# Moving casts from VectorE to ScalarE and GpSimd ahead of the attention units, and the order of a few small steps in a fused attention and expert kernel

## The reference

```python
x = x + xattn(layernorm(x), ctx)      # x: 4 x 1024 x 256, ctx: 4 x 64 x 192, 16 heads of 16
#   q = xn @ Wq + bq;  k = ctx @ Wk + bk;  v = ctx @ Wv + bv
#   softmax(clip(q k^T * scale, -1e4, 1e4)) @ v @ Wo + bo
#   (all probabilities become 1/64 if any of them is NaN)
x = x + ffn(layernorm(x))             # shared SwiGLU plus 8 experts of hidden size 512, top 2
```

## Time and profile before

| | |
|---|---|
| median of 3 runs | 696.8 us (696.21 to 697.24) |
| the profiled execution | 694.34 us, its span 692.6 us |
| PE busy | 606.9 us (88%) |
| DVE busy | 422.7 us (61%) |
| ACT busy | 344.7 us (50%) |
| POOL busy | 393.1 us (57%) |
| granted PE clock, mean | 0.926 |

### The profile page before, as it was taken

How to read it: one execution, slowest core, us unless ns; L and a number is a source line. 1 busy time by engine, 2 the same in 40 slices (tenths; PEclk the granted TensorE clock), 3 DMA queues, 4 the chain that set the end, 5 groups by cost and what they waited for, 6 DMA issues and landing times.

```text
span 692.6 us, 15435 instructions
## 1 busy us (share of the span) xinstructions
PE 606.9 (88%) x5212; PEld 413.3 (60%) x5212; DVE 422.7 (61%) x920; ACT 344.7 (50%) x567; POOL 393.1 (57%) x330
## 2 busy tenths in 40 slices
PE   3597688999987896998898999999999999999990
PEld 1243234565554563554665678778788878787870
DVE  5999974987785652889945444454444454444440
ACT  3986376786768762565145334243333333333330
POOL 6598588887662112432126544656666667656643
PEclk9999855997759998999999999999999999999996
DMA  8443302152118899595219764566575667665633
GB/s 266 88 77 76 130 1 33 32 139 44 35 25 191 160 185 292 145 175 146 69 54 175 122 91 73 101 98 105 90 115 86 100 97 103 100 100 86 101 41 37
DMA packets 121102, 72.44 MB, mean 105 GB/s; under 512 B 91779, under 2 KB 114246, under 8 KB 121030
## 3 DMA queue, kind: packets, MB, share of 16 engines
q1 hardware_dynamic: 101974, 44.01, 29.4%
q0 software_dynamic: 19056, 27.43, 24.8%
HBM read 29.47 MB, written 22.15 MB: 75 GB/s over the span
## 4 chain that ended last, share of the span: by engine, by line
PE 58%; DVE 16%; DMA 8%; SPq 6%; ACT 5%; issue 4%; POOL 2%; POOLq 0%; DVEq 0%; ACTq 0%
PE bank L1517 56%; SPq L547 4%; DVE bank L1116 3%; DMA out<-w_stage,map_i 3%; DVE arena L1063 2%; DMA arena<-arena 2%; DMA qx<-qx 2%; PE bank L1876 1%; ACT arena L809 1%; DVE arena L1180 1%; DVE hidden L1411 1%; DVE bank L1417 1%; POOL out L739 1%; DMA qx<-arena 1%; POOL arena L636 1%
## 5 line engine op out<-in xcount | busy, mean ns | idle before, releaser
L1517 PE MATMUL bank<-arena 128*128 128x34 f16 (+6 forms) x1282 | 139.7, 253 | 23.7 <-DVE bank L1116 7.9
L1517 PE MATMUL bank<-qx,arena 128*128 128x256 f16 (+1 forms) x1584 | 157.9, 290 | 2.8 <-ACT hidden L869 1.2
L739 POOL DMA_INDIRECT out<-w_stage,map_i x71 | 113.8, 1602 | 72.3 <-DMA out<-w_stage,map_i 37.1
L1517 PEld LDWEIGHTS bank<-qx,arena 128*128 (+1 forms) x1584 | 126.7, 102 | 24.4 <-issue 8.9
L1517 PEld LDWEIGHTS bank<-arena 128*128 128x128 f16 (+2 forms) x1282 | 77.5, 107 | 74.7 <-issue 41.3
L726 POOL DMA_INDIRECT qx<-rows_d,map_i x71 | 73.3, 1033 | 78.1 <-DVE lane_w L1478 35.7
L1486 DVE TENSOR_TENSOR hidden<-bank,hidden 128x512 f32<-128x512 f32 x71 | 49.1, 692 | 108.0 <-ACT hidden L995 108.0
L1517 PE MATMUL bank<-arena,w_stage 128*128 x852 | 104.7, 273 | 1.7 <-ACT w_stage L1001 1.2
L995 ACT ACTIVATE hidden<-bank 128x512 f32<-128x512 f32 x71 | 42.4, 597 | 126.9 <-PE bank L1517 126.9
L1517 PE MATMUL bank<-qx,w_sh 128*128 128x512 f16 x384 | 91.1, 384 | 9.8 <-DVE hidden L1411 7.5
L1517 PEld LDWEIGHTS bank<-arena,w_stage 128*128 128x128 f16 x852 | 82.0, 98 | 18.5 <-issue 4.7
(11 more groups left out here) (188 smaller groups left out, 716.6 us busy)
## 6 DMA issues: line engine op xcount, KB each, us to landing
w_stage<-in_w_all SPq DMA_DIRECT2D x27, 512.0 KB, 4.7
out<-x_sb POOLq DMA_DIRECT2D x16, 512.0 KB, 7.8
x_sb<-in_x SPq DMA_DIRECT2D x8, 512.0 KB, 7.5
rows_d<-arena SPq DMA_DIRECT2D x8, 512.0 KB, 3.9
qx<-rows_d,map_i POOLq DMA_INDIRECT x71, 3.2
qx<-qx SPq DMA_TRANSPOSE x71, 3.4
out<-w_stage,map_i POOLq DMA_INDIRECT x71, 4.1
arena<-arena SPq DMA_TRANSPOSE x56, 2.5
```

The lines of the kernel that those rows point to most:

```text
L739: pool.indirect_dma_start(out=out, out_offset=bass.IndirectOffsetOnAxis(ap=map_i[:, 1, i:i + 1], axis=0), in_=y_sb[:, r], in_offset=None, ...
L1517: return pe.matmul(o, a, b, start=first, stop=last, skip_group_check=not check)
```

## The change

- DVE's casts of Wo, gate and values go to ACT (behind `normal(7)`, `query(5)` and `query(6)`); the gate's low half goes to POOL. POOL's `values_low` and the low half of Wo come one group later.
- `exp_scale` is worked out behind the first clip of unit 0 and not ahead of it.
- Late scores 56 to 63 are taken one each in units 4 to 11, not 3 to 10. The clips of the last two groups of maxima go from DVE (units 1 and 10) to POOL (units 2 and 12, ahead of the first low half), as `clip_late`; the transposition and the copy of the last group come one unit later.
- The first steps and the last result of the second norm's reciprocal root are kept in PSUM, and a further instruction each copies `ve2` and `rstd2` to SBUF.
- A small tensor (`bo_hi`) lies in another buffer.

```diff
@@ late_scores
-            if 3 <= u < 11:
-                return range(LATE_MAX + u - 3, LATE_MAX + u - 2)
+            if 4 <= u < 12:
+                return range(LATE_MAX + u - 4, LATE_MAX + u - 3)
@@ POOL
-                if n == 4:
+                if n == 5:
+                    pool.wait_ge(gate_hi, 1)
+                    pool.tensor_tensor(gate_hl[:, :, 1], gate_f[:, :, :], gate_hl[:, :, 0],
+                                       ALU.subtract).then_inc(gate_split, 1)
                     pool.wait_ge(wo_hi, 1)
                     pool.tensor_tensor(wo_hl[:, 1], wo_f, wo_hl[:, 0], ALU.subtract).then_inc(wo_lo, 1)
-                if n == 5:
+                if n == 6:
                     pool.wait_ge(vh_ready, 1)
-                if n in (5, 6):
+                if n in (6, 7):
                     pool.wait_ge(ql_ready, HF * (n + 1))
-                    values_low(n - 5)
-                    pool.wait_ge(vblk_ready, n - 4)
+                    values_low(n - 6)
+                    pool.wait_ge(vblk_ready, n - 5)
+
+            def clip_late(n):
+
+                pool.wait_ge(smax_used, HF * GT * (n + 1))
+                pool.wait_ge(mt_ready, n - 1)
+                pool.tensor_scalar(m_cl[:, n % 2, :, :, 0:HD], m_raw[:, n % 2].unsqueeze(2).to_broadcast([P, GT, RT, HD]),
+                                   -CLIP, CLIP, ALU.max, ALU.min).then_inc(mcl_late, 1)
...
+                    if r == 0 and u in (2, 12):
+                        clip_late(NG - 2 if u == 2 else NG - 1)
@@ ACT
+                if n == 4:
+                    act.wait_ge(v_loaded, 16 * N_V)
+                    act.copy(wo_hl[:, 0], wo_f).then_inc(wo_hi, 1)
+                    act.copy(gate_hl[:, :, 0], gate_f[:, :, :]).then_inc(gate_hi, 1)
+                if n == 5:
+                    act.wait_ge(v_copied, B)
+                    act.copy(v_hh, v_f).then_inc(vh_ready, 1)
+                if n == 6:
+                    high_values()
@@ DVE
-                if n == 2:
-                    dve.wait_ge(v_loaded, 16 * N_V)
-                    dve.tensor_copy(wo_hl[:, 0], wo_f).then_inc(wo_hi, 1)
...
                 for r in range(RT):
                     clip(u, r)
+                    if u == 0 and r == 0:
+                        scale_of_exps()
@@ scale_guess2, scale_and_shift2
-                rsqrt_guess(dve, link2, mv2[:, t, 1], ve2[:, t], bits2[:, t], bank[7][:, t])
+                y, ve, bit = (bank[7][:, 64 * a:64 * a + NT][:, t] for a in range(3))
+                link2(dve.tensor_scalar(ve, mv2[:, t, 1], EPS, None, ALU.add))
+                link2(dve.tensor_scalar(ve2[:, t], ve, 1.0, None, ALU.mult), False)
+                link2(dve.tensor_scalar(bit.bitcast(I32), ve.bitcast(I32), 1, None, ALU.logical_shift_right))
+                link2(dve.tensor_scalar(y.bitcast(I32), bit.bitcast(I32), -1.0, MAGIC, ALU.mult, ALU.add))
...
+                link2(dve.tensor_scalar(rstd2[:, t], y, 1.0, None, ALU.mult), False)
+                dve.scalar_tensor_tensor(out=shift2[:, t], in0=mv2[:, t, 0], scalar=-1.0, in1=y,
@@ PE, max_t
-                pe.wait_ge(mcl_ready, n + 1)
+                if n < NG - 2:
+                    pe.wait_ge(mcl_ready, n + 1)
+                else:
+                    pe.wait_ge(mcl_late, n - NG + 3)
```

More of the change, by code:

```diff
@@ L152, in build @@
         bo_f = carve([C], F32, P // 2)
-        bo_hi = carve([C], F16, P // 2)
+        bo_hi = w_stage[0:P // 2, 3, 0:C // 2].bitcast(F16)
         ones_r = carve([P], F32, 1)
@@ L266, in build @@
         wo_lo = sem("wo_lo")
+        gate_hi = sem("gate_hi")
         gate_split = sem("gate_split")
@@ L290, in build @@
         mcl_ready = sem("mcl_ready")
+        mcl_late = sem("mcl_late")
         mt_ready = sem("mt_ready")
@@ L840, in copy_v, with high_values @@
                 act.copy(v_f[:, b], bank[7][:, 0:C]).then_inc(v_copied, 1)
+            def high_values():
+                act.wait_ge(vh_ready, 1)
+                for h2 in range(2):
+                    r = slice(h2 * KV, (h2 + 1) * KV)
+                    vh = v_hh[r].rearrange("p b (j h d) -> p b j h d", h=2, d=D)[:, :, :, h2, :]
+                    act.copy(v_blk_h[r, :, :, h2 * D:(h2 + 1) * D], vh).then_inc(vblk_hi, 1)
             normal(0)
@@ L1079, in copy_max @@
                                 bank[max_bank(n)][:, 0:256].bitcast(F16)).then_inc(mt_copied, 1)
[L1081 to L1085, removed]
             for n in range(NG - 2):
@@ L1092, in _, with scale_of_exps @@
                 clip_max(n)
-                if n == 2:
-                    dve.wait_ge(v_loaded, 16 * N_V)
-                    dve.tensor_copy(wo_hl[:, 0], wo_f).then_inc(wo_hi, 1)
[L1096 to L1111, removed]
+            def scale_of_exps():
+                dve.wait_ge(flag_ready, 1)
+                link(dve.tensor_reduce(flag[:, 0:1], bank[7][:, 0:HF * NG + HF], AX.X, ALU.add))
+                link(dve.tensor_tensor(flag[:, 1:2], flag[:, 0:1], flag[:, 0:1], ALU.is_equal))
+                dve.tensor_scalar(exp_scale, flag[:, 1:2], SCALE, None, ALU.mult).then_inc(scale_ready, 1)
             def clip(u, r):
@@ L1122, in late_max @@
                     row_max(j)
[L1123 to L1126, removed]
             def normalise(v):
@@ L1193, in unit @@
                     copy_max(NG - 2)
-                if u == 12:
+                if u == 13:
                     copy_max(NG - 1)
@@ L1219, in scale_guess2 @@
                 dve.wait_ge(ln2_link, seen2[0])
-                rsqrt_guess(dve, link2, mv2[:, t, 1], ve2[:, t], bits2[:, t], bank[7][:, t])
-                rsqrt_round(dve, link2, ve2[:, t], t2[:, t], bank[7][:, t], bank[7][:, t])
-            def scale_and_shift2(t):
-                rsqrt_round(dve, link2, ve2[:, t], t2[:, t], bank[7][:, t], bank[7][:, t])
-                rsqrt_round(dve, link2, ve2[:, t], t2[:, t], bank[7][:, t], rstd2[:, t])
-                dve.scalar_tensor_tensor(out=shift2[:, t], in0=mv2[:, t, 0], scalar=-1.0, in1=rstd2[:, t],
+                y, ve, bit = (bank[7][:, 64 * a:64 * a + NT][:, t] for a in range(3))
[3 more added lines that the diff above has]
+                link2(dve.tensor_scalar(y.bitcast(I32), bit.bitcast(I32), -1.0, MAGIC, ALU.mult, ALU.add))
+                rsqrt_round(dve, link2, ve2[:, t], t2[:, t], y, y)
+            def scale_and_shift2(t):
+                y = bank[7][:, t]
+                rsqrt_round(dve, link2, ve2[:, t], t2[:, t], y, y)
+                rsqrt_round(dve, link2, ve2[:, t], t2[:, t], y, y)
+                link2(dve.tensor_scalar(rstd2[:, t], y, 1.0, None, ALU.mult), False)
+                dve.scalar_tensor_tensor(out=shift2[:, t], in0=mv2[:, t, 0], scalar=-1.0, in1=y,
                                          op0=ALU.mult, op1=ALU.mult).then_inc(rstd_ready, 1)
@@ L1735, in unit @@
                     max_t(NG - 2)
-                if u == 11:
+                if u == 12:
                     max_t(NG - 1)
```

## The result

The changed kernel takes 689.6 us (median, 688.4 to 691.0) against 696.8 before: a ratio of 0.990, 95% interval 0.988 to 0.992, a gain of 7.2 us where 8.3 were forecast. Run again later, unaltered, beside 33 runs of the kernel before, it took 689.1 against 695.9: 0.992 (0.989 to 0.995). Ratios are of the fast runs alone, while the medians here are of all runs. The profiled executions differ by less than the medians: 694.34 before and 689.70 now, 4.6 us, where the prediction had this execution at 686.0.

What follows compares the result with a forecast made beforehand. DVE with its casts was taken to bound the first stage, then DVE's clips alternating with PE. Terms -6.5 + 0.3 - 2.3 + 0.2 = -8.3 us gave 696.8 - 8.3 = 688.5, range 684 to 692.5.

Steps and rivals of the forecast that it cites:

- The casts: First stage: without the casts on DVE, last maxima end near 76.5 instead of 81.19, 4.7 us gained; ACT's cost taken as 0.
- the last `query` still starts at 70.6: First stage: POOL and SP don't depend on the moved casts, so the last `query` starts no earlier than before, at 70.6.
- The clock in the last `query`: Last `query`, second half: the fall to 1.2 GHz was to go with the idle 2.93 us, part of the 4.7 us.
- Into unit 0: First exponential at 79.8, held by POOL's `values_low`, where it began at 84.24: 4.4 us earlier.
- Units 1 to 3: POOL decides, `clip_late` takes 0.6 us; unit 3's scores start at 97.3, 3.6 us earlier, behind a new 1.8 us wait.
- Late scores: Unit 3: the 2.96 us wait for the late score goes; unit 4's scores at 104.1, 6.5 us gained by there.
- The reciprocal root: Ahead of unit 15: PSUM operands spare DVE's steps waiting for POOL, 2.3 us gained; other 12 tiles cost 0.2.
- the gain should stay: Behind 235 us: nothing is tied to an absolute time, all waits for semaphores of the work ahead, so no loss.
- clock earlier up: Rival: shorter gaps in units 1 to 3 raise the clock about three units sooner, 1.6 us each: 683.7; chance 0.15.
- Half hidden: Rival: `clip_late` costs 1.15, ACT's casts uncovered, 1.6 us go; with the last `query`'s clock fall 3.6: 692.1; chance 0.17.
- Clock lower: Rival: new waits keep the clock low, units go from 5.9 to 7.5 us; with seven 699.7; chance 0.12.
- swallowed: Rival: SP's transposes and POOL's stores collide anew behind the units and end where they did, 696.5; chance 0.06.

Runs made afterwards that it cites:

- all three further changes together: Changed kernel with both late clips back on DVE, POOL's value low halves ahead of q's last, NaN-test sum read from PSUM: 689.9 us, ratio 0.991.
- values-ahead kernel: Changed kernel with both low halves of the values on POOL ahead of q's last low halves, NaN-test sum read from PSUM: 691.0 us, ratio 0.991.
- all four further changes: Changed kernel with late clips on DVE, values ahead, NaN sum from PSUM, DVE's first-weight low half behind unit 4's clips: 689.0 us against 696.4, ratio 0.989.

## Why the prediction held, point by point

- **The casts: right mechanism, size too large.** The last maxima were to end at 76.5 and ended at 77.3 and 78.1; 4.7 us were forecast, while the first profiles of the two kernels lie 3.1 apart and the second ones 4.4. The step "the last `query` still starts at 70.6" took the transposes as fixed; it started at 71.0 and 71.85, behind waits of 0.85 and 2.82 us for the DMA. Why the transposes came later stays open. Undoing the casts cost 3.5 to 4.2 us, putting them alone brought 2.1 to 2.6 up to the last maxima. ACT's cost was hidden as forecast: its five added instructions (0.61, 0.20, 1.05 and 1.26 for the two copies, 3.1 us) lie in free time, and in the first profile it still waited for PE 1.4 to 2.4 us at a time. What the prediction did not say: 2.15 of DVE's 5.4 us were the gate's two steps of 16 elements, which ended where POOL's instructions did (66.40 and 67.51, against POOL's 65.16 + 1.16 and + 2.32), so they were mostly waiting; the same two take 0.20 us on ACT and 0.21 on POOL.
- **The clock in the last `query`: right, but not sure.** Two matmuls and a score take 0.65 us there now, the price at the upper level (2.4 GHz), and the idle time of 2.82 us just ahead did not bring the clock down, unlike the 2.93 before. In all nine profiles with the changed kernel's casts but that of the casts alone the clock stood at 1.00 from 70 to 79. In six of them PE had waited 2.6 to 3.0 us for the transposes. In the other three (the changed kernel again, the root undone, all three further changes together) the clock had fallen one call earlier, to 0.50 from 66 to 68, and PE then waited only 0.8 to 1.0 us, so the transposes covered that loss. In the casts-alone kernel, whose PE does the same there, it fell after 2.52 us idle and cost 1.7 us. No length of the idle time tells these apart; what does stays open.
- **Into unit 0: right time, another releaser.** The first exponential started 3.1 us behind the last maxima; 79.8 - 76.5 = 3.3 was forecast. It was released by DVE's scale at 81.12 and not by POOL's values, which ended at 80.9. "DVE's scale ends near 78.5 and is not last" was wrong: the comparison again waited for POOL and took 1.07 us. It also held clips 1 to 3, so the later exponentials and all of POOL's list came later than forecast. The edit of the scale by itself costs 0.5 to 0.6 us.
- **Units 1 to 3: the failed size.** `clip_late` took 1.08 us, within the bounds of 0.5 to 1.15, but I had taken 0.6 by the element count; the row of any POOL instruction was the nearer one. With POOL's list 2 us late, unit 3's scores began at 99.53 and not 97.3: 1.4 us gained and not 3.6. The next step, 6.8 us on to unit 4's scores, was 6.75. So by unit 4 4.35 us were gained, 6.5 forecast. At these two places, unit 3's scores and unit 4's, the second profiles of the two kernels lie 2.9 and 5.9 us apart.
- **Late scores: right.** The wait of 2.96 us is gone, and undoing the part costs 2.4 us at unit 4: the wait, less the 0.6 that POOL's clip costs against DVE's. That cost was forecast as 1.8; DVE's clip waits for POOL in turn.
- **The reciprocal root: right where POOL's low halves fall on it.** 2.3 us forecast, 2.3 measured by undoing it; the 2.38 us of three first steps became 0.73 for four (184.09 to 184.82). But in two of five profiles with the root in SBUF the steps ran ahead of POOL, and there the part is worth 0.7 to 0.9 at most. The prediction took POOL's place from one profile and gave this no chance. For the other 12 tiles 0.2 us were to be lost; their steps took 3.1 us before and 2.7 now, since the last one, in SBUF, had taken 0.72.
- **What was not in the sum.** Between units 4 and 15 the first profile gained 4.1 us on before, 1.8 more than the 2.3 of the reciprocal root; the drift can give this, since the same kernel later gained only 0.5 there on the first profile of before. In the slots the first profile lost 3.7 us, which the sum held at 0 ("the gain should stay"). That is partly the spread, and perhaps partly `bo_hi`. So the first profiles lie 8.4 us apart at unit 15, nearly what the sum has (8.5), because 2.2 too little by unit 4 met 1.8 of drift; at the end they lie 4.6 apart. That the medians differ by 7.2, near the forecast 8.3, is in part luck: misses of 2 to 4 us to both sides cancel.

The rivals: "clock earlier up" did not come in the form told. The clock did rise for a moment at 86 us and came up at 117.7 to stay until 145, where it was 122.7 to 143, 5 us sooner but with the units 4.35 us sooner too. "Half hidden" came in part: `clip_late` at 1.08, but the casts were covered and the clock held. "Clock lower" and "swallowed" did not come in the changed kernel. The clock's fall in the last `query`, which "half hidden" holds, came in the casts-alone kernel.

## What to carry to other kernels

An engine with half its time free can still be the bound of one stage: ask of each small operation in its list who waits behind it, and move those whose inputs have long been ready to an engine that stands idle then. A gain ends where the next wait begins: here 5.4 us of work left DVE's list and up to 4.2 came back, the rest becoming waits for transposes. Where DVE and POOL are both busy on a chain, give each of DVE's short steps an operand in PSUM; a step of 0.18 us can cost over 1 otherwise. Whether it does depends on when POOL's instruction starts, so look at more than one profile before you price it.

## What the runs showed of the hardware

- Short DVE instructions whose operands all lie in SBUF took up to 1.2 us instead of 0.17 where they met a POOL instruction under way, and ended where POOL's ended (187.71, 188.83, 192.16); a weight's low half that takes 1.22 us took 2.77. Where POOL started later they took 0.17 (193.27, 193.47). Not each one was held: the one-element multiplication behind the comparison took 0.15 us at 81.01 in the values-ahead kernel, with POOL busy from 80.40 to 82.43. With one operand in PSUM the steps of the root took 0.15 to 0.19, whatever POOL did; the NaN comparison went from 1.07 to 0.15 us with POOL busy both times (here in the kernel with all four further changes):

```profile
80.18 0.15 DVE L1123 TENSOR_TENSOR arena<-arena,bank 128x1 f32<-128x1 f32 x1
```

  The Trainium skill, "SBUF — State Buffer", on who interferes with whom, says so of two SBUF inputs and of the two-port modes; these rows agree. The added cost that the Trainium skill gives a PSUM source in "VectorE: DVE Perf Modes", in the errata table, is not seen in them: 128x20 from SBUF took 0.17 us (193.27), from PSUM 0.17 to 0.18.
- A clip of 256 elements took POOL 1.08 us, about what 512 elements of a subtraction take (1.12 to 1.16): the element count was no guide.
- One program, with the same marks to within 0.9 us up to unit 4, took 79.2 us once and 82.7 once from there to unit 15, units falling into 5.9 or 7.5 us with the granted clock.
